# A first expert layer sorted by expert in place of one that runs every token through all eight experts, with the last gather behind the first tile's up products

## The chip, the cores and the metric

The kernel runs on one core of one Trainium2 chip. The metric is the device time of one execution in microseconds (us). A core has TensorE (PE, matrix products into the PSUM memory; PEld is its weight load), VectorE (DVE), ScalarE (ACT), GpSimd (POOL) and SyncE (SP, which issues most of the loads), and all of them use the on-chip memory SBUF. Matmul in float32 is written as two instructions in the records; `float32r` (fp32r) products are single.

## The reference, cut to what matters

A small vision tower on 16 images: a patch embedding to 36 tokens an image (576 tokens of width 192), then four pairs of a token mixer and a second layer, each on a normalised copy of the stream and added back to it. The change is in the second layer of pair 0: eight experts, one for each token.

```
x = layernorm(h).reshape(-1, 192)                  # 576 tokens
p = softmax(x @ router_w + router_b)               # 8 experts
e = argmax(p)                                      # one expert for a token
y = silu(x @ w1[e]) * (x @ w2[e])                  # 192 -> 512
h = h + max(p) * (y @ w3[e])                       # 512 -> 192
```

The order of the stages is attention 0, these experts (M0), a grid attention, attention 1, attention 2, experts M2 (8 and a shared one, top 2), attention 3, experts M3 (16, top 8).

## The kernel before

Every engine has a program of its own, written out by hand in one function; the engines meet through counted semaphores (`wait_ge`, `then_inc`). Each stage normalises the tokens in two halves of 288 (`layer_norm`, DVE; the power of the variance is on POOL), turns them on PE so that features lie on partitions (`turn`, lines 550 to 563), and copies them out of PSUM. The last turn and the last output products of a stage overlap with the first half of the next.

**The experts before.** `moe` (PE at lines 592 to 705, ACT at 1056, DVE at 1597, POOL at 1939) is shared by the three expert layers. It never gathers tokens. For M0 it goes through 8 experts x 2 halves x 4 chunks of 128 hidden features = 64 units. Products here are split: weights and tokens are each stored as a rounded high part and a low part in fp32r (`WH`, `WL`, `XH`, `XL`, and `X1`, that holds high and low of the last 64 features on the two halves of the partitions), and a unit's gate and its up product are five fp32r products each:

```
mm(o, WH[r][:, 0, w], XH[:, cols], start=True, stop=False)
mm(o, WH[r][:, 0, w], XL[:, cols], start=False, stop=False)
mm(o, WL[r][:, 0, w], XH[:, cols], start=False, stop=False)
mm(o, WH[r][:, 1, w], X1[:, cols], start=False, stop=False)
last = mm(o, WL[r][:, 1, w], X1[:, cols], start=False, stop=True)
```

ACT takes the silu of the gate, DVE multiplies by the up part, POOL multiplies by a 0/1 row that is 1 where the token belongs to the expert (`spread_both` makes these rows), ACT and DVE split the result into high and low (`AH`, `AL`), and `down` (line 649) adds five more fp32r products to a sum in PSUM. ACT (`up_high`, `down_high`) and DVE (`up_low`, `down_low`) split each expert's weights one expert ahead; those of expert 0 are split inside attention 0. Weights come through two pairs of buffers, `RG` and `RD`, that SP fills (`slots`). DVE also does `centre(n)` in this stage, twelve pieces of work on the weights of attention 1. At the end `by_tokens` turns the sums back, and `stream` adds them, times the largest probability, to `H`. `keep_clock` puts products with no use on PE while it would wait in the grid stage.

Of the kernel before, what the change touches and what calls it, by code (L numbers as in the profile page):

```python
# [33 lines left out]
NC_ = 2  # L34
CR = (128, C - 128)
CB = (CR[0], CR[1] + 1)
TP = 96
# [100 lines left out]
MOES = [M0, M2, M3]  # L138
A0.then, A1.then, A2.then, A3.then = M0, None, M2, M3
# [5 lines left out]
SG0 = {M0.name: 0, M2.name: M0.units}  # L145
AM0 = {m.name: sum(x.weighted(u) for x in MOES[:i] for u in range(x.units)) for i, m in enumerate(MOES)}
SLOTS = [(m, s) for m in MOES for s in range(m.slots)]
RING = 2
PARTS = 9
WG_ = 1024  # L150
GRP = 14
STAGES = [("attn", A0), ("moe", M0), ("grid", None), ("attn", A1), ("attn", A2), ("moe", M2), ("attn", A3), ("moe", M3)]
# [6 lines left out]
YN = [sum(1 for k, _ in STAGES[:i] if k != "moe") for i in range(len(STAGES) + 1)]  # L159
# [61 lines left out]
def bass_vit_tower(nc, t, out):  # L221
    with ExitStack() as ctx:
# [40 lines left out]
        rstd = sb("rstd", [TP, NG])  # L263
        cst = sb("cst", [128, 128])
# [40 lines left out]
        TX2 = over("TX2", [TP, TAU * 256], F32)  # L305
        WH = [sb("WH0", [128, NC_, WG_], F32R)]
        WL = [sb("WL0", [128, NC_, WG_], F32R)]
        DW = [sb("DW0", [128, 4, 2 * C], F32R)]
# [5 lines left out]
        with ExitStack() as place:  # L314
# [8 lines left out]
            TX = [sb1(f"TX{r}", [TP, TAU * 256]) for r in range(2)] + [TX2]  # L323

# [46 lines left out]
        def turned_by_time(j, c, lo, hi):  # L371

            return turned(j, c, lo, hi).rearrange("k (t b m) -> k t b m", t=TAU, b=HB)

        XH = sb("XH", [128, B * N], F32R)
# [4 lines left out]
        DW.append(sb("DW1", [128, 4, 2 * C], F32R))  # L380
        AH = [sb(f"AH{r}", [128, HN], F32R) for r in range(PARTS)]
# [17 lines left out]
            "dve_step", "pool_step",  # L399
        )}  # L400
        in_att = {n: sem("in_att_" + n) for n in ("l0a", "grid", "l1f", "l2a", "l3a")}
        in_w2 = [sem(f"in_w2_{k}") for k in range(3)]
# [59 lines left out]
        def _(sp):  # L462
# [38 lines left out]

            qkv(A0)
            proj(A0)
            slots(M0, 0, RING)
# [6 lines left out]
            slots(M0, RING, M0.slots)  # L511
            slots(M2, 0, RING)
# [34 lines left out]
        def _(pe):  # L547
# [27 lines left out]
            def router(i, e, stage, j):  # L575

                wait_xt(stage, j)
                if j == 0:
                    pe.wait_ge(S["x_split"], 2 * MOES.index(STAGES[stage][1]) + 1)
# [7 lines left out]
            def keep_clock(n, bank):  # L587

                for _ in range(n):
                    mm(PS[:, bank, 0:HN], WH[0][:, 0, 0:128], WH[0][:, 0, 128:128 + HN], start=True, stop=True)  # L590

            def moe(m, stage):
# [88 lines left out]
                for u in range(m.units + m.lag):  # L681
# [4 lines left out]
                    if u == 1:  # L686
                        if m is M3:
                            keep_clock(11, 7)
                        turn(stage, 1)
# [12 lines left out]
                if stage + 1 < len(STAGES):  # L702
                    keep_clock(14, 0)
                    turn(stage + 1, 0)
                by_tokens(1)

# [219 lines left out]
            def grid_attention(stage):  # L926
# [16 lines left out]
                for j in range(2):  # L943

                    keep_clock((27, 41)[j], 7)
# [33 lines left out]
            for i, (kind, arg) in enumerate(STAGES):  # L979
                if kind == "moe":  # L980
                    moe(arg, i)
                elif kind == "attn":
# [1092 lines left out]
```

## Time and profile before

| | us |
|---|---|
| median of 3 runs | 718.22 (717.99 to 719.23) |
| the profiled execution | 716.98 |
| its span, first to last instruction | 714.4 |
| PE busy in it | 678.0 |
| stage M0, first split product to the turn for the grid | 84.6 to 229.7 |

The trace holds one execution. Starts are microseconds from the span's first instruction. The time of an execution also holds what lies before and behind the span, 2.6 us here.

### The profile page before, as it was taken

Reading aid. Unit: us, or ns where it says so; the run is one execution under the profiler, and the core shown is the slowest. Engines: PE = TensorE matmul, PEld = TensorE weight load, DVE = VectorE, ACT = ScalarE, POOL = GpSimd, SP = SyncE. Lnnn points to the kernel's source line nnn. Section 1 sums busy time; section 2 is a strip of 40 time slices with the busy share of each in tenths; the row PEclk is TensorE's granted clock in tenths of the full one; section 3 lists DMA queues with packets and bytes.
Section 4 is the critical chain, followed back from the end, with each engine's and each line's share of the span. In section 5 each row is a group of like instructions: output and inputs, shape, how many; then the busy total and the mean of one; then the engine's idle time right before and its main releaser. Section 6 shows DMA issues by size and latency. Waiting matters only on the chain.

```text
span 714.4 us, 16229 instructions
## 1 busy us (share of the span) xinstructions
PE 678.0 (95%) x6345; PEld 616.3 (86%) x6345; DVE 486.0 (68%) x1198; ACT 366.3 (51%) x851; POOL 166.4 (23%) x164
## 2 busy tenths in 40 slices
PE   6999998999999999999999999999999998999996
PEld 6788898999998687799879998889999867889995
DVE  2658568888868882878774554677766747466785
ACT  0357454555543213588735753455454458357662
POOL 1200017444451202344122000054443120000000
PEclk9999999999999999999999999999999999899999
DMA  9932022222212000011100010212312100112000
GB/s 258 268 80 83 3 60 80 84 82 82 67 61 68 1 0 1 3 45 46 47 2 1 2 47 2 61 46 62 122 61 60 56 1 12 44 52 82 24 23 25
DMA packets 16891, 39.40 MB, mean 55 GB/s; under 512 B 3693, under 2 KB 4685, under 8 KB 16624
## 3 DMA queue, kind: packets, MB, share of 16 engines
q1 hardware_dynamic: 14840, 37.29, 17.9%
q10 hardware_dynamic: 1976, 1.08, 0.6%
q8 instruction: 50, 0.82, 0.5%
q14 instruction: 25, 0.20, 0.1%
HBM read 37.90 MB, written 0.44 MB: 54 GB/s over the span
## 4 chain that ended last, share of the span: by engine, by line
PE 73%; DVE 13%; ACT 7%; issue 5%; DMA 1%; POOL 1%; POOLq 0%; DVEq 0%; ACTq 0%; SPq 0%
PE PS L865 6%; PE PS L807 6%; PE PS L732 5%; PE PS L741 4%; PE PS L611 4%; PE PS L615 4%; PE PS L614 4%; PE PS L613 4%; PE PS L612 4%; DVE AL L1616 3%; PE PS L828 3%; PE PS L663 3%; PE PS L667 2%; PE PS L666 2%; PE PS L665 2%
## 5 line engine op out<-in xcount | busy, mean ns | idle before, releaser
L1065 ACT ACTIVATE MIX<-PS 128x288 f32<-128x288 f32 x118 | 48.4, 411 | 114.7 <-PE PS L615 114.5
L611 PE MATMUL PS<-XH,WH 128*128 128x288 f32 x284 | 86.3, 304 | 3.5 <-DVE OT L1605 1.4
L614 PE MATMUL PS<-X,WH 128*128 128x288 f32 x284 | 83.7, 295 | 0.0
L613 PE MATMUL PS<-XH,WL 128*128 128x288 f32 x284 | 83.7, 295 | 0.0
L615 PE MATMUL PS<-X,WL 128*128 128x288 f32 x284 | 83.7, 295 | 0.0
L612 PE MATMUL PS<-XL,WH 128*128 128x288 f32 x284 | 83.6, 295 | 0.0
L1927 POOL TENSOR_TENSOR rstd<-var,nhalf 96x3 f32<-96x3 f32 x18 | 17.2, 957 | 277.0 <-DVE var L1343 277.0
L1605 DVE TENSOR_TENSOR OT<-MIX,PS 128x288 f32<-128x288 f32 x94 | 42.3, 450 | 39.0 <-ACT MIX L1065 38.3
L1616 DVE TENSOR_TENSOR AL<-OT,AH 128x288 fp32r<-128x288 f32 x118 | 58.9, 507 | 3.3 <-ACT AH L1079 2.3
L1459 DVE TENSOR_TENSOR WL<-RG,WH 128x768 fp32r<-128x768 f32 (+2 forms) x46 | 57.8, 1258 | 3.5 <-ACT WH L1045 3.3
L611 PEld LDWEIGHTS PS<-XH,WH 128*128 128x128 f32 x284 | 53.5, 188 | 6.5 <-DVE OT L1605 1.9
L663 PE MATMUL PS<-AH,DW 128*128 128x288 f32 x166 | 52.3, 315 | 7.2 <-DVE AL L1616 7.0
L1949 POOL TENSOR_TENSOR OT<-OT,BIG 128x288 f32<-128x288 f32 x48 | 45.7, 964 | 51.9 <-DVE OT L1605 35.9
L612 PEld LDWEIGHTS PS<-XL,WH 128*128 128x128 f32 x284 | 53.5, 188 | 0.0
L614 PEld LDWEIGHTS PS<-X,WH 128*128 128x128 f32 x284 | 53.5, 188 | 0.0
L613 PEld LDWEIGHTS PS<-XH,WL 128*128 128x128 f32 x284 | 53.5, 188 | 0.0
L615 PEld LDWEIGHTS PS<-X,WL 128*128 128x128 f32 x284 | 53.5, 188 | 0.0
L1079 ACT ACTIVATE AH<-OT 128x288 fp32r<-128x288 f32 x118 | 50.2, 436 | 2.2 <-DVE OT L1611 2.2
L666 PE MATMUL PS<-AL,DW 128*128 128x288 f32 x166 | 49.0, 295 | 0.0
L665 PE MATMUL PS<-AH,DW 128*128 128x288 f32 x166 | 48.9, 295 | 0.0
L664 PE MATMUL PS<-AH,DW 128*128 128x288 f32 x166 | 48.9, 295 | 0.0
L667 PE MATMUL PS<-AL,DW 128*128 128x288 f32 x166 | 48.9, 295 | 0.0
(257 smaller groups left out, 1707.5 us busy)
## 6 DMA issues: line engine op xcount, KB each, us to landing
RG<-in_gu_l0f_dram SPq DMA_DIRECT2D x8, 512.0 KB, 4.3
RG<-in_gu_l0f_dram SPq DMA_DIRECT2D x16, 256.0 KB, 5.8
RG<-in_gu_l2f_dram SPq DMA_DIRECT2D x9, 384.0 KB, 3.6
RG<-in_gu_l2f_dram SPq DMA_DIRECT2D x18, 192.0 KB, 4.3
RD<-in_wd_l0f_dram SPq DMA_DIRECT2D x8, 384.0 KB, 3.3
RD<-in_wd_l2f_dram SPq DMA_DIRECT2D x9, 288.0 KB, 2.8
RD<-in_wd_l3f_dram SPq DMA_DIRECT2D x6, 384.0 KB, 3.1
BIG<-in_patch_dram SPq DMA_DIRECT2D x6, 288.0 KB, 7.7
```

The lines of the kernel that those rows point to most:

```text
L611: mm(o, WH[r][:, 0, w], XH[:, cols], start=True, stop=False)
L612: mm(o, WH[r][:, 0, w], XL[:, cols], start=False, stop=False)
L613: mm(o, WL[r][:, 0, w], XH[:, cols], start=False, stop=False)
L614: mm(o, WH[r][:, 1, w], X1[:, cols], start=False, stop=False)
L615: last = mm(o, WL[r][:, 1, w], X1[:, cols], start=False, stop=True)
L663: mm(FB(j, 0), W[:, 0:128], hi, start=first, stop=False)
L665: mm(FB(j, 1), both, hi, start=first, stop=False)
L666: mm(FB(j, 0), W[:, 0:128], lo, start=False, stop=final)
L667: mm(FB(j, 1), both, lo, start=False, stop=final).then_inc(S["w3_done"], 1)
L1079: activation(AH[I % PARTS][:, :], af(m, u), ACT.Copy).then_inc(S["ah_hi"], 1)
L1459: V.tensor_tensor(WL[r][:, part, 0:m.width], RG[r][:, part, 0:m.width], WH[r][:, part, 0:m.width].bitcast(F32), ALU.subtract).then_inc(S[" ...
L1616: V.tensor_tensor(AL[I % PARTS][:, :], af(m, u), AH[I % PARTS][:, :].bitcast(F32), ALU.subtract).then_inc(S["ah_lo"], 1)
```

## The change

The stage `("moe", M0)` becomes `("sorted", None)`. M0 goes from the list of shared expert layers, and with it the splits in attention 0. The new stage is a function of each engine:

1. The router's mask is multiplied by a triangle of ones and by ones (`ranks`), which gives each token its rank among the tokens of its expert; DVE makes a place of it (`positions`): tile e for the first 128 tokens of expert e, and one of four spare tiles (8 to 11) for what goes beyond 128. There are T0 = 12 tiles of S0 = 128 places.
2. `picked(n)` compares the places with a row 0 to 511 and gives a 0/1 matrix for each group of 96 tokens; `gather(n)` multiplies high and low parts of the tokens by it: 512 places at a time, features on partitions. Gather 0 and 1 (tiles 0 to 7) come first; gather 2 (the spare tiles) stands at `i == LATE`, behind tile 0's gate and up products.
3. For each tile: gate and up, 512 columns each, in full float32 with the weights as the moving operand; silu; product; four turns; a down product in float32.
4. `back` brings the rows to token order with 0/1 matrices (`PTT`) made on DVE, high and low parts in fp32r.
5. SP loads experts 0 to 3 into four rings ahead of attention 0's end and 4 to 7 as the rings come free. The weights of the spare tiles depend on the data: `owners` finds their expert, and POOL issues indirect loads.
6. `centre(i)` is done once a tile, and the useless products in the grid stage use `CT` instead of `WH`.

```diff
-MOES = [M0, M2, M3]
-A0.then, A1.then, A2.then, A3.then = M0, None, M2, M3
+MOES = [M2, M3]
+A0.then, A1.then, A2.then, A3.then = None, None, M2, M3
+E0, T0, S0, RING0 = 8, 12, 128, 4
+HID0 = 512
+RANKS = S0 * T0 // HID0
+GATHER = [4, 6, 0]
+LATE = 1
...
+            def expert(e):
+                r = e % RING0
+                if e >= RING0:
+                    sp.wait_ge(S["m0_up"], e - RING0 + 1)
+                sp.dma_start(GU[r], t["gu_l0f"][128 * e:128 * (e + 1), :]).then_inc(m0_in[r], 16)
+                if e >= RING0:
+                    sp.wait_ge(S["m0_down"], e - RING0 + 1)
+                sp.dma_start(WD[r], t["wd_l0f"][128 * e:128 * (e + 1), :]).then_inc(m0_in[r], 16)
...
+            for e in range(RING0, E0):
+                expert(e)
+            for r in range(RING):
+                sp.wait_ge(S["m0_up"], E0 + r + 1)
+                sp.wait_ge(S["m0_down"], E0 + r + 1)
+                slots(M2, r, r + 1)
...
+            def sorted_experts(stage):                                   # PE
+                def gather(n):
+                    for g in range(NG):
+                        pe.wait_ge(S["m0_picked"], NG * n + g + 1)
+                        for part, c in ((0, 0), (1, 0), (2, 1)):
+                            last = mm(PS[:, GATHER[n] + c, 0:HID0], XNS[:, g, 128 * part:128 * (part + 1)], PM[:, n % 2, g, :],
+                                      start=(g == 0 and part != 1), stop=(g == NG - 1 and part != 0), skip_group_check=True)
+                    last.then_inc(S["m0_gathered"], 1)
...
+                def up(i):
+                    if i < E0:
+                        pe.wait_ge(m0_in[i % RING0], 32 * (i // RING0 + 1))
+                    else:
+                        pe.wait_ge(m0_over[i - E0], 32)
+                    pe.wait_ge(S["m0_xs"], 2 * (i * S0 // HID0 + 1))
+                    if i == LATE:
+                        pe.wait_ge(S["m0_xs"], 2 * RANKS)
+                    if i >= 2:
+                        pe.wait_ge(S["m0_h"], i - 1)
+                    w = GU[i % RING0].rearrange("p (c f) -> p c f", c=2)
+                    for k in range(2):
+                        for c in range(2):
+                            last = mm(PS[:, up_bank(i) + k, 0:HID0], XS[:, c, i * S0:(i + 1) * S0], w[:, c, k * HID0:(k + 1) * HID0],
+                                      start=(c == 0), stop=(c == 1))
+                    last.then_inc(S["m0_up"], 1)
...
+                turn(stage, 1)
+                for j in range(2):
+                    router(*ROUTER["l0f"], stage, j)
+                ranks()
...
+                for n in range(RANKS - 1):
+                    gather(n)
+                for i in range(T0 + 2):
+                    if i == LATE:
+                        gather(RANKS - 1)
+                    if i < T0:
+                        up(i)
+                    if i == 0:
+                        positions()
+                    if 0 <= i - 1 < T0:
+                        turn_hidden(i - 1)
+                    if 0 <= i - 2 < T0:
+                        down(i - 2)
+                for j in range(2):
+                    back(j)
+                turn(stage + 1, 0)
...
+                for n in range(RANKS - 1):                               # ACT
+                    sorted_rows(n)
+                for i in range(T0 + 2):
+                    if i == LATE:
+                        sorted_rows(RANKS - 1)
+                    if i < T0:
+                        silu(i)
...
+                positions(view(3, 0, E0))                                # DVE
+                for n in range(RANKS):
+                    picked(n)
+                diagonals()
+                owners()
+                for i in range(T0 + 2):
+                    if i < T0:
+                        hidden(i)
+                    if 0 <= i - 2 < T0:
+                        low_out(i - 2)
...
+                            back(n)
+                    if i < T0:
+                        centre(i)
+                largest(M0, view)
...
+                if kind == "sorted":                                     # POOL
+                    for n_ in range(T0 - E0):
+                        b = (E0 + n_) % RING0
+                        if n_ == 0:
+                            pool.wait_ge(S["m0_index"], 1)
+                        pool.wait_ge(S["m0_up"], E0 - RING0 + n_ + 1)
+                        at = bass.IndirectOffsetOnAxis(ap=oidx[:, n_:n_ + 1], axis=0)
+                        G.indirect_dma_start(GU[b], None, t["gu_l0f"], at).then_inc(m0_over[n_], 16)
+                        pool.wait_ge(S["m0_down"], E0 - RING0 + n_ + 1)
+                        G.indirect_dma_start(WD[b], None, t["wd_l0f"], at).then_inc(m0_over[n_], 16)
```

`ranks` is 12 float32 products with 8 to 48 columns; `positions` on PE is 6 float32 products with 96 columns, and on DVE 11 small linked operations; `picked(n)` is 6 operations of 96 partitions x 512 and `back` on DVE one of 128 x 576; `turn_hidden` is 4 turns of 128 x 128; `down` is 4 float32 products with 192 columns; `back` on PE is 72 fp32r products with 192 columns for each half.

## Rows read from the trace of the kernel before

**Rows 1.** Windows of attention 0 and of stage M0: busy time (instructions) of each engine.
```profile
core 0: us, PE busy (x) PEld busy (x) DVE busy (x) ACT busy (x) POOL busy (x), PEclk, DMA share, GB/s
22.00:84.60 62.60, 60.91 (x888) 50.61 (x885) 39.40 (x110) 34.37 (x85) 4.34 (x3) 1.00 0.40 108
84.60:229.70 145.10, 140.97 (x1041) 136.27 (x1041) 115.79 (x256) 72.75 (x166) 62.18 (x66) 1.00 0.24 72
```

**Rows 2.** Timeline of PE around the start of stage M0: start us, us.
```profile
80.47 0.38 PE L559 MATMUL PS<-cst,XN 96*128 96x96 f32 x2
...
82.35 0.94 PE L865 MATMUL PS<-wp_l0a,OT 96*96 96x192 f32 x4
...
86.26 1.11 PE L582 MATMUL PS<-wr,XT 128*96 128x8 f32 x12
...
91.50 0.29 PE L611 MATMUL PS<-XH,WH 128*128 128x288 f32 x1
...
92.15 0.29 PE L611 MATMUL PS<-XH,WH 128*128 128x288 f32 x1
```

**Rows 3.** The chain that ended last, several stages: start us, us, what.
```profile
50.15 0.37 PE PS L838 x4
...
69.91 3.97 PE PS L865 x24
...
224.37 0.55 DVE MIX L1685
...
229.72 0.71 PE PS L559 x6
...
231.23 6.07 PE PS L939 x24
...
250.49 3.09 PE PS L957 x18
...
608.11 7.52 PE PS L865 x24
```

**Rows 4.** Timeline of VectorE and GpSimd in stage M0: start us, us.
```profile
84.62 0.56 DVE L1705 TENSOR_TENSOR H<-PS,H 96x384 f32<-96x384 f32 x1 [0.19 <-PE PS L865]
...
87.85 0.95 DVE L1350 TENSOR_SCALAR XN<-H,mv,rstd 96x192 f32<-96x192 f32 x3 [0.96 <-POOL rstd L1927]
...
94.75 0.20 DVE L1486 TENSOR_REDUCE rs<-PS 96x6 f32<-96x48 f32 x1
...
97.03 0.50 DVE L1544 MAX8 top<-rl 96x8 f32<-96x8 f32 x6
...
99.37 0.19 DVE L1562 TENSOR_SCALAR CB<-rl 96x48 fp32r<-96x48 f32 x1
...
208.12 7.17 POOL L1949 TENSOR_TENSOR OT<-OT,ACC 128x288 f32<-128x288 f32 x8 [1.01 <-DVE OT L1605]
...
211.64 0.99 DVE L1593 TENSOR_TENSOR wqkv_l1f<-wqkv_l1f,cw 65x256 f32<-65x256 f32 x1
```

**Rows 5.** Groups by form over the whole span, DVE and ACT: busy us, mean ns.
```profile
L1706 DVE TENSOR_TENSOR H<-PS,H 96x192 f32<-96x192 f32 x10 | 3.4, 344 | 0.0
...
L1593 DVE TENSOR_TENSOR wqkv_l1f<-wqkv_l1f,cw 128x256 f32<-128x256 f32 x6 | 2.6, 426 | 0.2
...
L1213 ACT ACTIVATE PT<-PS 128x432 f32<-128x432 f32 x16 | 8.3, 520 | 13.0 <-PE PS L838 13.0
```

**Rows 6.** Windows near the end of attention 3, columns as in the first group.
```profile
606.00:608.00 2.00, 1.20 (x30) 0.99 (x22) 1.90 (x6) 1.98 (x7) 0.00 (x0) 1.00 0.66 197
610.00:612.00 2.00, 2.00 (x8) 1.78 (x7) 1.78 (x6) 0.44 (x1) 0.00 (x0) 0.50 0.22 86
```

**Rows 7.** Loads: issues, KB each, median us from issue to landing.
```profile
RG<-in_gu_l0f_dram SPq DMA_DIRECT2D x16, 256.0 KB, 5.8
...
RD<-in_wd_l0f_dram SPq DMA_DIRECT2D x8, 384.0 KB, 3.3
```

**Rows 8.** A window of the start, with loads queued, columns as in the first group.
```profile
28.00:32.00 4.00, 4.00 (x24) 2.90 (x23) 3.21 (x6) 2.08 (x5) 2.15 (x1) 1.00 1.08 261
```

More of the change, by code:

```diff
@@ L148 @@
 RING = 2
+E0, T0, S0, RING0 = 8, 12, 128, 4
[3 more added lines that the diff above has]
+LATE = 1
+BLOB = dict(zip(("iota", "above", "ones", "thr", "kth", "eth", "base", "over", "slot", "part"),
+                np.cumsum([0, HID0, 128, 128, 32, 32, 32, E0, E0, T0]).tolist()))
+BLOB_W = BLOB["part"] + 1
 PARTS = 9
@@ L158 @@
 TAKEN = [2 * sum(1 for k, _ in STAGES[:i] if k == "attn") for i in range(len(STAGES) + 1)]
-YN = [sum(1 for k, _ in STAGES[:i] if k != "moe") for i in range(len(STAGES) + 1)]
+YN = [sum(1 for k, _ in STAGES[:i] if k not in ("moe", "sorted")) for i in range(len(STAGES) + 1)]
 XV_N = {"l0a": 0, "l1f": 1, "l2a": 2, "l3a": 3}
@@ L305, in bass_vit_tower @@
         TX2 = over("TX2", [TP, TAU * 256], F32)
+        GU = [RG[r][:, :, :].rearrange("p c f -> p (c f)") for r in range(RING)]
+        WD = [RD[r][:, :] for r in range(RING)]
+        GU.append(over("GU2", [128, 2 * WG_], F32)[:, :])
         WH = [sb("WH0", [128, NC_, WG_], F32R)]
+        GU.append(over("GU3", [128, 2 * WG_], F32)[:, :])
         WL = [sb("WL0", [128, NC_, WG_], F32R)]
+        WD2 = over("WD2", [128, 2, 4 * C], F32)
+        WD += [WD2[:, r, :] for r in range(2)]
         DW = [sb("DW0", [128, 4, 2 * C], F32R)]
@@ L323, in bass_vit_tower, with const0, scratch0, up_bank @@
             TX = [sb1(f"TX{r}", [TP, TAU * 256]) for r in range(2)] + [TX2]
+        XS = OT[:, 0:2 * S0 * T0].rearrange("p (c n) -> p c n", c=2)
+        HB0 = [BIG[:, r * HID0:(r + 1) * HID0] for r in range(2)]
+        HT0 = [BIG[:, 1920 + r * HID0:1920 + (r + 1) * HID0] for r in range(2)]
+        SG0B = [MIX[:, r * HID0:(r + 1) * HID0] for r in range(2)]
+        POST = XT[:, 0, :]
+        DIAG = ACC[0:TP, :, 0:TP]
+        def const0(name, n, rows=128):
+            return BIG[0:rows, 1024 + BLOB[name]:1024 + BLOB[name] + n]
+        def scratch0(o, n, rows=128):
+            return BIG[0:rows, 2944 + o:2944 + o + n]
+        POS = scratch0(176, NG * RANKS, TP).rearrange("p (n g) -> p n g", n=RANKS)
+        def up_bank(i):
+            return 2 * ((i + 1) % 2)
         def af(m, u):
@@ L577, in router @@
                 wait_xt(stage, j)
-                if j == 0:
+                if j == 0 and STAGES[stage][0] == "moe":
                     pe.wait_ge(S["x_split"], 2 * MOES.index(STAGES[stage][1]) + 1)
@@ L981, in _ @@
                     moe(arg, i)
+                elif kind == "sorted":
+                    sorted_experts(i)
                 elif kind == "attn":
@@ L1440, in second_half_in @@
                         w2_split(4 + part)
-                if a is A2:
+                if a is A2 or kind == "sorted":
                     return
@@ L1881, in _ @@
                     moe(arg, i)
+                elif kind == "sorted":
+                    sorted_experts(i)
                 elif kind == "attn":
@@ L2010, in moe, with put @@
         t["wd_" + m.name] = down.reshape(m.slots, m.chunks, 128, C).transpose(0, 2, 1, 3)
-    moe(M0, a["L0_ffn_w1"], a["L0_ffn_w2"], a["L0_ffn_w3"])
+    w = np.concatenate([a["L0_ffn_w1"], a["L0_ffn_w2"]], axis=2)
+    t["gu_l0f"] = np.concatenate([w[:, 0:128], np.concatenate([w[:, 128:C], w[:, 128:C]], axis=1)], axis=2).reshape(E0 * 128, 2 * WG_)
+    t["wd_l0f"] = a["L0_ffn_w3"].reshape(E0, 4, 128, C).transpose(0, 2, 1, 3).reshape(E0 * 128, 4 * C)
+    blob = z(128, BLOB_W)
+    def put(name, x):
+        x = np.asarray(x, f)
+        blob[:, BLOB[name]:BLOB[name] + x.shape[-1]] = x
+    put("iota", np.arange(HID0))
+    put("above", np.triu(np.ones((128, 128)), 1))
+    put("ones", np.ones(128))
+    put("thr", np.tile(S0 * np.arange(1, 5), E0))
+    put("kth", np.repeat(np.arange(4), E0))
+    put("eth", np.tile(np.arange(E0), 4))
+    put("base", S0 * np.arange(E0))
+    put("over", S0 * E0 - S0 - S0 * np.arange(E0))
+    put("slot", np.arange(128)[:, None] + S0 * np.arange(T0))
+    put("part", np.arange(128)[:, None])
+    t["m0c"] = blob
     cat = lambda w, s: np.concatenate([s[None], w]).transpose(0, 2, 1)
```

242 lines of the change are left out of this document (212 added, 30 removed).

## The prediction

> **What bounds the kernel now.** I read the stage table first. In the stage that the change rewrites (84.6 to 229.7 us, 145.1 us long) PE is busy for 140.97 us at granted clock 1.00, VectorE for 115.8, ScalarE for 72.8, and the DMA engines for 24% [rows 1]. The stage in front of it is PE's as well. So PE's own work sets this stage. It is 64 units of 15 products over 288 columns: 128 gate and up groups of five and 64 down groups of five. Five such products, each with other weights, start within 0.65 us (91.50 to 92.15), so the pace is 0.131 us a product, not the 0.29 us of one [rows 2]. 960 x 0.131 = 126 us; the rest is turns, router, spreads of weights and short waits. The chain of waits then gives the paces of the full float32 products, each of which leaves two records [rows 3]: 12 of 288 columns in 6.07 us and 9 of 192 columns in 3.09 us, 0.506 and 0.343 us each, 1.7 ns a column and 0.017 besides; so 0.886 for 512 columns.
>
> **The change removes** those 126 us and the stage's weight splits. Attention 0 loses six ACT and DVE splits too, worth nothing there: its stretch shows PE busy 60.9 of 62.6 us, so PE hides them [rows 1].
>
> **It adds a chain before the first sorted tile.** Nothing fills PE there; each link is on the path.
> 1. The half turn in front of the stage does three products fewer than before (the second-half copies are made only for the other expert stages): 80.47 to 82.35 before, now 0.71 as for the grid [rows 2, 3]. The last output product is then 1.2 us earlier: 83.4 instead of 84.6.
> 2. Residual add to normalised rows: 84.62 to 88.80, 4.2 us [rows 4]: 87.6. Turn, 0.8: 88.4.
> 3. Router, two halves of 12 records at 1.1 us [rows 2], and 0.1 to DVE: 90.7. The second half's copies (0.4 us) lie behind the first half's products.
> 4. Shift, eight-largest, mask: 0.4, and 2.5 less 0.8 for a product of hidden values in between [rows 4]: 92.8.
> 5. Rank products: 12 float32, 24 records. Router records of 8 columns take 1.11/12 = 0.09 us, so their weights set the pace; I take 0.10: 2.4, to 95.2. The low parts of the sorted rows are made on DVE meanwhile.
> 6. Eleven linked small DVE operations. A reduce over 96x48 takes 0.20 [rows 4]; 0.22 with the link: 2.4, to 97.6.
> 7. Selection matrices: 18 DVE operations of 512 columns. The nearest is the normalising operation with per-partition scalars, three of 192 columns in 0.95 us, 0.32 each [rows 4]; at one element a cycle 512 columns are 0.65. If only one scalar lets the operation go at twice that, 0.4. I take 0.65 as the row has no faster form. PE needs 3 products of 512 columns for each, 3 x 0.225 = 0.68 from the 0.131 for 288. So both engines are nearly equal, and the two early ranks end at 97.6 + 12 x 0.68 + 0.9 (the first pick and hops) = 106.7, whichever price holds.
> 8. Tile 0's products, 4 x 0.886 = 3.55 (110.2). DVE is still at the third rank (97.6 + 18 x 0.65 and 0.4 for offsets: 109.7) and the diagonals (six at 0.2, and a hop): 111.2. The product of positions is queued on PE ahead of the third gather and waits for this: 1.0 us idle, and 1.2 of work: 112.4. With picks at 0.4 this wait goes.
> 9. Third gather, 6 x 0.68 = 4.1, then ScalarE empties its two banks, 0.6 each (128x432 takes 520 ns [rows 5]), and tile 1 waits for it: 117.8. That is where this kernel puts the spare tiles' rows. Behind the waiting product on PE are tile 0's turn and down products; DVE and ScalarE have nothing else due, so 1.3 us of idle PE is the price.
>
> **Then the tiles**, PE after PE: 11 x 3.55 for up products, 12 turns of 0.45 (four of 108 columns 0.37 [rows 3]), 12 down products of 4 x 0.343 = 1.37: 60.9 us, to 178.7. A tile is 5.4 us. ScalarE needs 0.6 + 0.6 + 0.35 for it; DVE 0.7 (hidden), 0.35 (low part, 344 ns for 192 columns), 2 x 0.72 (positions back), 1.05 (one piece of centring, its long part 426 ns) = 3.5 [rows 5]. Both fit. The last tile's latency behind a table load: 1.0, to 179.7. The return: 144 products of 192 columns at 0.131 x 192/288, and 0.004 for a fixed part: 0.0915 each, 13.2 us, to 192.9. The grid stage's turn follows at once: it needs 5.3 us after the first half's sum (224.37 to 229.72 [rows 3]), and the second half's 6.6 us of products cover it. Hops between engines not yet counted: 1.0. So the turn that was at 229.7 stands at 193.9.
>
> **Two costs that this leaves out.** The clock: between 90.7 and 98 PE has 2.4 us of work in 7.3. After a stretch with PE busy 1.20 of 2.00 us the granted clock fell from 1.00 to 0.50 (2.4 to 1.2 GHz) and 24 output records took 7.52 us for 3.97 before [rows 3, 6]: 3.5 us lost. I take that here, for the gathers. Below stands nothing (no drop); above, a second drop at the wait after 116.5, 7.
>
> The spare tiles' weights: POOL issues them as indirect loads, 1024 KB up and 384 KB down. The down set of tile 8 waits for tile 4's down product, the end of one tile's time, and is needed 5.4 us later; each next one likewise, with the next tile's up set queued ahead of or behind it. On SP 384 KB land in 3.3 us and the last of an expert's up loads 5.8 us after its issue [rows 7], at some 260 GB/s when the engines are full [rows 8]; one tile's two sets, 1.44 MB, need 5.5 us at that. No row shows an indirect load. Bounds: as SP's, 0 us; or each late by its queue mate's 4 us less what is spare, about 3 us a tile, 12 in all. I take 2, nearer SP's rows.
>
> By the Trainium skill (DMA: Bandwidth & Descriptors, "Anatomy of one DMA — SWDGE (gpsimd) path") a load issued from GpSimd takes 2.0 us and its bytes at 436 GB/s; the estimate for 384 KB is then 2.9 us, near the row's 3.3, and the sum would be 2 us lower. No trace here shows such a load.
>
> **The sum.** 229.7 - 193.9 = 35.8; less 3.5 and 2: 30.3 us saved. The profiled execution took 716.98 (span 714.40): 686.7. The median of the runs is 1.24 above it: 688.
>
> **The rivals.**
> - *Clock held, loads in time.* 35.8 saved: 682.4; with fast picks another 1 less. For it: the stretch of 1.20 busy itself still stood at 1.00 [rows 6]. Against: seven microseconds at a third busy is more idle than what came before that fall.
> - *The spare loads bind.* 3 us a tile more than slack, 12: 698 in place of 688 (10 above my 2). For it: 1.44 MB in 5.4 us is the full rate [rows 8]. Against: DMA is otherwise idle (24%). A mechanism that would bring it: DVE and POOL hold each other up in SBUF. DVE's centring operation on 256 columns took 0.99 us while POOL multiplied, 426 ns on the mean of its kin [rows 4, 5], and here DVE is busy 3.5 of 5.4 us; if POOL writes its descriptors only in DVE's gaps, a load of 5 becomes 8.5, 3.1 over the slot, four times. The Trainium skill (SBUF — State Buffer, "SBUF: two separate sides") states such a rule: a VectorE operation in a two-port mode locks GpSimd out, and loads issued there starve for descriptors. The trace shows the lock for computing operations, none for a load.
> - *Slower than before.* The same loads decide: at more than 5.4 + 32.3/4 = 13.5 us from issue to landing for each of the four down sets, the 30.3 us and my 2 are gone; at 14 us, 720. Nothing in the trace is that slow at 384 KB (3.3), so it needs descriptors that are made one by one.
> - *The products are cheaper than costed*, the return bound by less than 0.09: under 680.
>
> **How the numbers follow.** Forecast 0.50 (684 to 693), clock and loads well 0.15 (680 to 684), loads bind 0.27 (693 to 708), slower 0.03, no change 0.01, under 680 0.04. To leave out no more than 2 in 10 the range goes from 680 to 701: outside are 0.04 below, about 0.08 of the load case, and 0.04. A measurement of this kernel tells 0.2% from nothing, 1.4 us: faster 0.96, same 0.01, slower 0.03.
>
> **What the profile after would show.** Right: no group of the split products before the grid; up products at 0.44 us a record; 3.55 us from one tile's first up product to its turn, and 5.4 from tile to tile; PE idle 1.3 us before tile 1's products, released by ScalarE; the granted clock at 0.50 for a few us near 98; the grid's turn near 199. Wrong: PE waiting on a DMA of the expert weights ahead of tiles 8 to 11 for more than 1 us each; a tile longer than 6 us, with DVE or ScalarE as releaser; gather slower than 0.7 us a group, bound by DVE.

## The result, and the profile after

The changed kernel took 683.81 us (median of 4 runs, 682.27 to 687.89), the kernel before 718.64 beside it (717.99 to 719.23). The ratio is 0.9524, 95% interval 0.9482 to 0.9567. In two later measurements of six runs each the changed kernel took 683.95 and 683.97 us, 0.9537 (0.9497 to 0.9577) and 0.9527 (0.9487 to 0.9567). Of the six runs of e10_mid below one is left out of its figures as slow: it took 691.24 us at a mean granted clock of 0.963, the others 675.98 to 678.71 us at 0.984 to 0.990. The profiled execution took 682.27 us, with a span of 680.5.

The windows of attention 0 and of the new stage answer to [rows 1]; columns are the span's stretch, its length, busy time (instructions) of PE, PEld, DVE, ACT and POOL, the granted clock, the DMA share and GB/s.

```profile
core 0: us, PE busy (x) PEld busy (x) DVE busy (x) ACT busy (x) POOL busy (x), PEclk, DMA share, GB/s
22.00:83.40 61.40, 59.69 (x882) 50.08 (x880) 35.89 (x105) 30.57 (x80) 4.35 (x3) 1.00 0.41 134
83.40:198.30 114.90, 102.88 (x506) 75.41 (x507) 52.20 (x172) 24.77 (x49) 9.77 (x10) 0.90 0.38 128
```

PE's work in the stage fell from 141.0 to 102.9 us, VectorE's from 115.8 to 52.2, ScalarE's from 72.8 to 24.8. But PE now has 12 us without work, where it had 4, and the mean granted clock is 0.90, where it was 1.00. The chain that ended last shows the order of the stage (start us, us, what), where [rows 3] had the split products:

```profile
81.29 2.10 PE PS L1043 x12
...
86.65 0.97 DVE XN L1586 x3
87.66 1.22 PE PS L621 x6
88.88 3.71 PE PS L644 x24
...
97.70 2.57 PE PS L792 x12
103.38 11.43 PE PS L776 x36
114.81 3.44 PE PS L818 x8
118.25 1.31 PE PS L800 x12
119.56 4.17 PE PS L776 x18
123.75 1.09 ACT OT L1254 x2
124.97 3.67 PE PS L818 x8
...
160.39 5.12 DMA RD<-in_wd_l0f_dram,oidx
...
185.36 12.96 PE PS L856 x144
```

L644 is the router, L792 the second kind of rank products, L776 a gather, L818 the up products, L800 `positions`, L856 the return. From tile 1 to the return every link is PE's but for two places: a load of the spare tiles (160.39 to 165.51), and ScalarE in front of the last down product (181.4 to 183.8), where it loads the table of its exponential (e5). PE's waits in 80 to 200 us (waited for: us in total, times, longest):

```profile
PE PS L621 <- DVE XN L1586: 4.3, 1, 4.3
PE PS L776 <- DVE PM L1945: 3.1, 1, 3.1
PE PS L785 <- DVE rl L1805: 2.4, 1, 2.4
PE PS L818 <- ACT OT L1254: 1.3, 1, 1.3
...
PE PS L841 <- ACT BIG L1241: 0.7, 1, 0.7
PE PS L818 <- DMA RD<-in_wd_l0f_dram,oidx: 0.3, 1, 0.3
```

The first three are the router's chain: normalised rows, places, mask. The fourth is the price of the gather's place. The last is the whole price of the spare tiles' loads. The windows of PE's clock (columns as above) show what the three long waits set off:

```profile
82.00:86.00 4.00, 1.38 (x9) 1.10 (x7) 2.17 (x9) 0.04 (x1) 0.23 (x1) 0.99 0.00 0
86.00:90.00 4.00, 2.34 (x15) 2.35 (x16) 2.14 (x6) 1.19 (x3) 0.61 (x1) 0.50 0.01 4
102.00:106.00 4.00, 2.62 (x6) 2.18 (x7) 3.83 (x13) 0.00 (x0) 0.00 (x0) 0.50 0.00 0
106.00:110.00 4.00, 4.00 (x11) 3.13 (x10) 1.87 (x6) 0.00 (x0) 0.00 (x0) 0.52 0.00 0
110.00:114.00 4.00, 4.00 (x20) 3.29 (x19) 3.17 (x11) 1.08 (x2) 0.00 (x0) 1.00 0.00 0
```

PE was busy 1.38 of 4 us, then the clock stood at 0.50 (1.2 GHz) through turn, router, ranks and the first 6.4 of the 11.4 us of the early gathers, 24 us long, and came back near 109.8 us, when PE had been busy without a pause from 103.4 us.

**Where the 33.9 us of the span came from.** The grid's turn stands at 198.32 for 229.72: 31.4. Later turns of PE stand at 335.99 for 366.64, at 409.94 for 440.53 and at 540.91 for 571.49, 30.6 to 30.7 earlier. The next one stands at 588.31 for 622.22, 33.9 earlier. These last 3.3 us can't be put down to the change: before, the clock fell to 0.50 at 608 us [rows 6], and in this execution it did not at the same place:

```profile
578.00:582.00 4.00, 4.00 (x27) 3.86 (x26) 3.13 (x9) 0.44 (x1) 0.00 (x0) 1.00 0.26 95
```

In e1, e4 and e10 below, whose edits all lie in the expert stage, it did fall there. Here is e4:

```profile
576.00:578.00 2.00, 2.00 (x10) 1.85 (x10) 1.97 (x5) 0.48 (x2) 0.00 (x0) 0.50 0.76 185
```

### The profile page after: what moved, and what is told of

It is laid out like the page before. It is cut to its first block, busy times and chain, and to the rows that moved or that the text cites. A ratio compares the mean times of both kernels' runs of the same rounds, so it can differ in the third digit from the quotient of the medians.

```text
span 680.5 us, 14646 instructions
## 1 busy us (share of the span) xinstructions
PE 635.9 (93%) x5793; PEld 552.9 (81%) x5793; DVE 418.6 (62%) x1109; ACT 314.5 (46%) x730; POOL 114.0 (17%) x108
## 4 chain that ended last, share of the span: by engine, by line
PE 74%; DVE 12%; ACT 7%; issue 4%; DMA 1%; POOL 1%; POOLq 0%; DVEq 0%; SPq 0%; ACTq 0%
PE PS L985 6%; PE PS L818 6%; PE PS L910 6%; PE PS L1043 6%; PE PS L919 4%; PE PS L1006 3%; PE PS L673 2%; PE PS L776 2%; PE PS L1146 2%; PE PS L1033 2%; PE PS L677 2%; PE PS L675 2%; PE PS L676 2%; PE PS L674 2%; PE PS L841 2%
## 5 line engine op out<-in xcount | busy, mean ns | idle before, releaser
L673 PE MATMUL PS<-XH,WH 128*128 128x288 f32 x156 | 48.1, 308 | 3.3 <-DVE OT L1848 1.4
L674 PE MATMUL PS<-XL,WH 128*128 128x288 f32 x156 | 46.0, 295 | 0.0
L676 PE MATMUL PS<-X,WH 128*128 128x288 f32 x156 | 46.0, 295 | 0.0
L675 PE MATMUL PS<-XH,WL 128*128 128x288 f32 x156 | 46.0, 295 | 0.0
L677 PE MATMUL PS<-X,WL 128*128 128x288 f32 x156 | 45.9, 295 | 0.0
L725 PE MATMUL PS<-AH,DW 128*128 128x288 f32 x102 | 32.0, 313 | 4.4 <-DVE AL L1859 4.2
L910 PE MATMUL PS<-wqkv_l1f,XT 128*96 128x256 f32 (+1 forms) x144 | 34.3, 387 | 0.8 <-ACT XT L1194 0.8
L1702 DVE TENSOR_TENSOR WL<-RG,WH 128x768 fp32r<-128x768 f32 (+1 forms) x30 | 31.0, 1037 | 3.4 <-ACT WH L1280 3.3
L910 PEld LDWEIGHTS PS<-wqkv_l1f,XT 128*96 128x96 f32 (+1 forms) x144 | 29.1, 209 | 2.5 <-issue 1.0
L728 PE MATMUL PS<-AL,DW 128*128 128x288 f32 x102 | 30.1, 295 | 0.0
L726 PE MATMUL PS<-AH,DW 128*128 128x288 f32 x102 | 30.1, 295 | 0.0
L727 PE MATMUL PS<-AH,DW 128*128 128x288 f32 x102 | 30.1, 295 | 0.0
L729 PE MATMUL PS<-AL,DW 128*128 128x288 f32 x102 | 30.1, 295 | 0.0
```

Source lines behind the costliest of these rows:

```text
L725: mm(FB(j, 0), W[:, 0:128], hi, start=first, stop=False)
L726: mm(FB(j, 0), W[:, 256:384], hi, start=False, stop=False)
L910: last = mm(PSF[0:TP, 1024 + tau * 2 * a.fq:1024 + (tau + 1) * 2 * a.fq], tile(XT[0:CB[c], c, 0:B * N], j, tau), W[0:CB[c], c, g * 2 * a.f ...
L1702: V.tensor_tensor(WL[r][:, part, 0:m.width], RG[r][:, part, 0:m.width], WH[r][:, part, 0:m.width].bitcast(F32), ALU.subtract).then_inc(S[" ...
```

## The experiments

A stage is measured here from the start of the half turn in front of it to the start of the grid's turn (117.6 us in the trace above). The rest is the span without it.

| run | stage | rest | time, us | what |
|---|---|---|---|---|
| after | 117.6 | 562.9 | 683.81 (4 runs) | the change |
| a0_after | 117.2 | 563.7 | 683.95 (6 runs) | the same |
| e1_late0 | 116.7 | 565.8 | 685.13 (6 runs) | last gather ahead |
| e2_first_fill | 113.7 | 566.3 | 681.77 (1 run) | one filling |
| e3_all_fill | 110.4 | 566.5 | 679.62 (6 runs) | three fillings |
| e4_pos_behind | 115.4 | 567.2 | 686.97 (6 runs) | positions behind the gather |
| e6_plain | 117.5 | 572.7 | 691.95 (1 run) | plain loads |
| e8_dve_copies | 116.3 | 567.8 | 685.83 (1 run) | copies on VectorE |
| e9_no_spare | 87.4 | 570.5 | 659.61 (1 run) | no spare tiles |
| a1_after | 117.1 | 566.0 | 683.97 (6 runs) | the same |
| e5_exp_late | 115.7 | 566.5 | 683.91 (1 run) | table load later |
| e7_all | 110.2 | 566.1 | 677.43 (6 runs) | e3, e4, e5 together |
| e10_mid | 109.2 | 567.8 | 676.88 (5 runs) | e7, fillings placed otherwise |

The column of the rest moves by 5 us without an edit there (e6 and e9: 8 to 10), so an edit in this stage is read from its stage first. What differs there between the traces is the clock, at places that no edit touched. The half turn in front of the stage starts at 79.4 to 80.6 us where the clock held until then. It starts at 81.9 to 82.6 us in the traces of a1, e2, e3, e7 and e8, where the clock stood at 0.50 for some 3.4 us from 24 or 25 us on, and at 84.0 in e6, where it did so for 7. Behind the grid's turn the clock falls to 0.50 for 2 to 7 us at two to five places (near 310 to 330, 400, 576, 672 and 682 us; in e6 near 240 as well; e9 has seven places). The three traces of the changed kernel, the same program, differ in this as well, by 3.1 us of the rest. So it changes from execution to execution, and one trace does not tell whether an edit has a share in it.

**a0_after.** The changed kernel unedited.

> The changed kernel again, on the same chip as the next three, so that they can be compared with it and not only with the kernel before. Every theory: 682 to 688 us; granted clock 0.50 from about 86 to 110 us, and the first up product at about 115.

It gave 683.95 (682.5 to 689.4). The clock was at 0.50 from 85 to 108 us, and the first up product stands at 113.1; the half turn started 1.1 us earlier than in the first trace.

**e1_late0: the place of the gather.**

```diff
-LATE = 1
+LATE = 0
```

> LATE = 0: the spare tiles' rows are gathered ahead of tile 0. Theory (PE order is what counts): the gather of 4.2 us and the 1.2 us in which ScalarE empties it lie ahead of tile 0 in place of tile 1, so the wait only moves, 0 us; but the position product then stands behind tile 0 with nothing to wait for, as before: within 0.5 us of the changed kernel. Rival (the place of the gather is what the change is worth): 1 to 4 us slower, because VectorE's third rank of matrices and the diagonals are no longer covered by tile 0's products, and are waited for.

685.13 (684.2 to 686.18), ratio to before 0.9544 (0.9512 to 0.9576), against 0.9537 (0.9497 to 0.9577) for the control. The stage is 0.5 us shorter, of which 0.3 is a wait for a spare load that the control had and this execution had not. The time is the same within the intervals; they alone would still leave room for the rival's lower end, 1 us, and the stage rules it out. Timeline of PE, three gathers in a row and then tile 0's up products:

```profile
102.75 15.26 PE L776 MATMUL PS<-PM,XNS 96*128 96x512 f32 x54 [3.13 <-DVE PM L1945]
119.28 3.67 PE L818 MATMUL PS<-RG,OT 128*128 128x512 f32 x8 [1.27 <-ACT OT L1254]
```

The wait for ScalarE's copies is the same 1.27 us, ahead of tile 0 and not of tile 1. VectorE's third rank of matrices and the diagonals, on which the rival rested, are waited for nowhere. Having the last gather behind tile 0 saves nothing as it stands: the wait only moves.

**e4_pos_behind: something between the gather and its user.** `positions` (PE) and its copy (ScalarE) go behind the last gather.

```diff
                     if i == LATE:
                         gather(RANKS - 1)
+                        positions()
                     if i < T0:
                         up(i)
-                    if i == 0:
-                        positions()
```

> The product of positions moves from behind tile 0's up products to behind the last gather, in ScalarE's order too. Theory: it then lies in the 1.2 us in which PE waits for ScalarE to empty the gather's banks; that wait goes, and the time falls by 1.0 to 1.3 us. Rival: tile 0's silu and product, and with them its turn, come behind the emptying and the copy of the positions on ScalarE (0.6 + 0.65 us), and PE waits for them instead: no change.

```profile
116.59 4.70 PE L776 MATMUL PS<-PM,XNS 96*128 96x512 f32 x18
121.12 1.47 PE L800 MATMUL PS<-ACC,BIG 96*128 96x96 f32 x12
122.55 3.67 PE L818 MATMUL PS<-RG,OT 128*128 128x512 f32 x8
```

The wait of 1.27 us is gone, and the stage is 1.7 us shorter than the control's; 0.3 of that is the control's wait for a load. The time is not: 686.97 (684.3 to 689.44), ratio 0.957 (0.9535 to 0.9606). Behind the grid's turn windows of 2 us show the clock at 0.50 for some 20 us in sum, for some 12 in the control. So the mechanism in the stage is shown, and in the whole the forecast gain of 1.0 to 1.3 us did not show: the median is 3.0 us above the control's, with intervals that overlap.

**e2_first_fill and e3_all_fill: the clock.** Useless products with `CT` in PE's waits, 30 ahead of the second half's turn, 16 ahead of the ranks, 21 behind them; e2 has the first 30 alone.

```diff
+                keep_clock(30, 7, CT)
                 turn(stage, 1)
                 for j in range(2):
                     router(*ROUTER["l0f"], stage, j)
+                keep_clock(16, 7, CT)
                 ranks()
+                keep_clock(21, 7, CT)
```

> Only the first of the three fillings: 30 products with no use while the last rows are normalised; the waits behind the router and the rank products stay empty. Theory (the clock falls in the 4.3 us wait for the normalised rows, and stays low because the rest of the chain is thin): it now falls later, near 92 to 98 us, so that the turn (0.7) and the router (2.0) are at the full clock and the ranks and early gathers are not; 2 to 3 us of the fillings' gain. Rival (once past the first wait the clock holds): all of it, first up product about 3 us earlier still.

> Products with no use are put on PE in its three waits at the start of the stage: 30 (3.9 us at the full clock) while the last rows are normalised, 16 (2.1) behind the router, 21 (2.7) behind the rank products. Theory (the clock costs about 8 us, not the 3.5 I had put): granted clock 1.00 throughout, turn 0.65 for 1.22 us, router 2.0 for 3.7, ranks 2.6 for 5.3, early gathers 8.2 for 11.4; first up product near 106, time 7 to 9 us below the changed kernel. Rival (the clock costs little, as VectorE's small operations and matrices bound the chain): less than 4 us.

In e2 the clock no longer fell at 86 us but in the next wait, behind the router:

```profile
90.00:92.00 2.00, 2.00 (x25) 1.91 (x23) 0.46 (x2) 0.49 (x2) 0.00 (x0) 1.00 0.00 0
92.00:94.00 2.00, 0.01 (x1) 0.00 (x0) 1.78 (x21) 0.00 (x0) 0.00 (x0) 0.80 0.00 0
```

From 93 to 107 us it was at 0.50. Turn and router took 0.72 and 2.13 us, the ranks as long as without a filling (2.27 and 2.71 for the two kinds), and the stage is 3.5 us shorter, a little over what was expected. So the wait for the normalised rows is what set off the first fall, and the next wait sets off one by itself.

e3 took 679.62 (677.42 to 681.89), ratio 0.947 (0.9435 to 0.9505): 4.3 us under the control on the same chip, with a stage 6.8 us shorter. The intervals overlap by 0.0008; the slowest of its six runs is 0.6 us faster than the fastest of the control's. PE's timeline in e3:

```profile
89.47 0.71 PE L621 MATMUL PS<-cst,XN 96*128 96x96 f32 x6 [0.34 <-DVE XN L1589]
90.02 2.13 PE L644 MATMUL PS<-wr,XT 128*96 128x8 f32 x24
...
94.81 1.25 PE L788 MATMUL PS<-rl,BIG 96*128 96x40 f32 x10
95.92 1.79 PE L792 MATMUL PS<-rl,BIG 96*128 96x8 f32 x12
97.56 4.27 PE L652 MATMUL PS<-CT 128*128 128x288 f32 x21
101.67 8.38 PE L776 MATMUL PS<-PM,XNS 96*128 96x512 f32 x36
```

The same 24 router records take 2.13 us for 3.90 without fillings, and the early gathers 8.38 for 11.43. From the half turn to the first gather it is 19.3 us for 22.8. Against the first trace of the changed kernel the stage is 7.2 us shorter, and 3.5 and 3.1 of them lie in these two stretches: the loss to the clock in the changed kernel is at least some 7 us.

The theory's "granted clock 1.00 throughout" did not come: the clock fell once more, at 97 us, and was back near 100.4. The filling behind the ranks took 4.27 us, not the 2.8 that 21 products need at full clock, and so it ran past its wait. VectorE began the first matrix of 0s and 1s at 100.21 us, the gather can start 0.63 us later (102.75 and 103.38 in the changed kernel), and it started at 101.67, 0.8 us late. The chain that ended last goes through the useless products themselves:

```profile
97.71 4.12 PE PS L652 x21
```

The timed gain of 4.3 us is between the theory's and the rival's bound, since the rest of the span gave 2.8 us back: the half turn of this execution starts 2.9 us later than the control's, behind the fall of the clock near 25 us that no edit touches.

**e5_exp_late: the table load.** ScalarE's exponential goes two tiles on.

```diff
-                    if i == T0 - 1:
+                    if i == T0 + 1:
                         router_exp(0, NG * E0, TP)
```

> ScalarE's exponential for the router stands two tiles later, behind the last hidden rows. Theory: the 0.7 us that PE waited for ScalarE at the last turn of hidden values was its table load of 1.3 us, ahead of the last silu; it goes, and the stage is 0.7 us shorter (116.4 to 117.0 us). Rival: the silu needs a table load of its own again or the wait belongs to the last tile's latency, and it stays at 0.5 us or more. Either way too little for one time to tell; the trace decides.

The wait of the last down products is gone: the last two tiles' 16 records follow each other, where a wait of 0.72 us for ScalarE splits them in a1_after, the control on the same chip.

```profile
179.58 2.77 PE L841 MATMUL PS<-WD,BIG 128*128 128x192 f32 x16
```

The cause is the table load, but not where the expectation has it. In the changed kernel it stands behind the last silu (179.64) and ahead of the copy of the last turned hidden values (183.17):

```profile
181.72 1.28 ACT L1371 ACT_TABLE_LOAD   x1
```

The stage is 1.5 us shorter than that control's; 0.7 is this wait, and 0.5 is a wait for the last tile's load, which this execution did not have and the control had.

**e6_plain: indirect or plain loads.** POOL's loads of the spare tiles fetch experts 0 to 3 by a fixed address.

```diff
-                        G.indirect_dma_start(GU[b], None, t["gu_l0f"], at).then_inc(m0_over[n_], 16)
+                        G.dma_start(GU[b], t["gu_l0f"][128 * n_:128 * (n_ + 1), :]).then_inc(m0_over[n_], 16)
```

(and the same for `WD[b]`).

> The spare tiles' weights come as plain loads of fixed experts from the same POOL queue at the same places, in place of indirect ones, so tokens in spare tiles get the weights of a fixed expert. Theory (indirect loads cost no more than plain ones here): landing within 0.5 us of 5.1 us after issue, no more than 0.3 us of PE waiting for them, stage length unchanged. Rival (indirect loads are what makes the down set of a tile arrive at the last moment): landing near 3.3 us, as SP's.

POOL's timeline for the second down set, first the changed kernel, then e6:

```profile
160.39 1.03 POOL L2292 DMA_INDIRECT RD<-in_wd_l0f_dram,oidx  x1 [2.90 <-PE PS L841]
```

```profile
164.25 0.55 POOL L2292 DMA_DIRECT2D RD<-in_wd_l0f_dram  x1 [4.07 <-PE PS L841]
```

The address from SBUF costs 0.4 to 0.5 us of POOL per load, and the down sets land a median 4.5 and 3.8 us after their issue (two each in `RD` and `WD`), 4.0 and 3.6 when plain. Each of the four landed 0.1 to 0.5 us sooner when plain; the second, the one that PE waited for, after 4.6 us for 5.1. So the indirect address is not what makes that set late, and the rival is refuted. The stage is as long as before the edit, 117.5: nothing hangs on it but the last 0.3 us of wait, which is gone here. The time of 691.95 is no measure of the loads: the half turn started 3.4 us later, and the rest of the span was the longest of all runs.

**e8_dve_copies: VectorE beside POOL's loads.** Four copies of 96x576 on VectorE in each of tiles 5 to 10.

```diff
+                    if 5 <= i < 11:
+                        for _ in range(4):
+                            link(V.tensor_copy(XN[:, 0:TAU, 0:C], XN[:, TAU:2 * TAU, 0:C]))
```

> VectorE makes four more copies of 96x576 from SBUF to SBUF in each of tiles 5 to 10, about 2 us of work in its slack while POOL issues the spare loads. Theory (the loads are bound by the DMA queue, not by VectorE): POOL's issue stays at 0.94 to 1.18 us, the down sets land within 0.5 us of before, PE waits under 1 us. Rival (VectorE's two-port copies keep GpSimd from writing descriptors): issues of 1.5 us and more, landings later by 1 to 3 us, PE waits 1 to 3 us for each of tiles 8 to 11.

Two of POOL's issues with the copies nearest to them:

```profile
157.77 0.94 POOL L2293 DMA_INDIRECT RG<-in_gu_l0f_dram,oidx  x1 [0.30 <-issue]
158.68 2.31 DVE L2014 COPY XN<-XN 96x576 f32<-96x576 f32 x4
...
168.03 1.29 POOL L2293 DMA_INDIRECT GU<-in_gu_l0f_dram,oidx  x1 [0.30 <-issue]
168.16 2.32 DVE L2014 COPY XN<-XN 96x576 f32<-96x576 f32 x4
```

The copies added 2.2 us to each tile. The down sets land after 4.2 and 3.8 us, and PE waits for no load in the stage, as the theory said. But the rival was hardly put to the test: the copies stand in the gaps between POOL's issues, as in the first two lines, and only one issue of eight lies beside them, the one at 168.03. It took 1.29 us, the same one of the changed kernel 1.03, and its load landed after 6.4 us, for 6.3 there. The other seven took as long as before, 0.94 to 1.18 us. So a hold-up of an issue by VectorE's work is neither shown nor refuted; what is shown is that this much more of it costs PE nothing. The Trainium skill (SBUF — State Buffer, "SBUF: two separate sides") says that a load issued from GpSimd has its descriptors held up while such float32 copies run; the 0.26 us of the one issue would agree, and its landing shows no delay. Whether these copies took both ports no row tells.

**e9_no_spare: what the spare tiles cost.** The four spare tiles are left out, with the third gather, their loads and their part of the return; tokens beyond 128 of an expert are dropped.

```diff
+TN = 8
...
-                for i in range(T0 + 2):
-                    if i == LATE:
-                        gather(RANKS - 1)
-                    if i < T0:
+                for i in range(TN + 2):
+                    if i < TN:
...
-                    for n_ in range(T0 - E0):
+                    for n_ in range(0):
```

> The four spare tiles are left out, with their gather, their loads and their part of the return; tokens beyond 128 of an expert are dropped. Theory (the stage is PE's sum of terms): 4 x 5.17 for the tiles, 4.17 + 1.25 for the gather and the emptying, 48 x 0.09 = 4.3 for the return: 30.4 us shorter. Rival (the start chain and hops bind, so that terms don't add): less than 25 us.

The stage takes 87.4 us, 30.2 less than in the first trace with them (29.8 less than in a0_after), for 30.4 expected: the terms add. Only 96 products of return remain:

```profile
157.16 8.88 PE L855 MATMUL PS<-YS,PTT 128*96 128x192 f32 x96
```

**a1_after, e7_all, e10_mid: the edits together.** The three ran on the same chip. e7 has the edits of e3, e4 and e5. e10 is e7 with

```diff
+                    keep_clock(8, 7, CT)
                     for g in range(NG):
                         last = mm(PS[:, 6, 0:E0], const0("ones", 128, TP), mask[:, g, :], start=(g == 0), stop=(g == NG - 1))
...
-                keep_clock(21, 7, CT)
+                keep_clock(17, 7, CT)
```

> The changed kernel once more, as the measure for the runs beside it: 682 to 687 us, ratio to the kernel before near 0.953. The stage from the half turn in front of it (first turn of six) to the grid's turn takes 117 to 118 us, with the granted clock at 0.50 for some 24 us of it.

> Three edits together: the useless products of 30, 16 and 21 in the stage's idle places, the product of positions moved behind the last gather, and ScalarE's exponential (a table load) moved two tiles later. My theory (what the stage lost to the clock and to two waits is separate and adds): in the stage -6.6 to -7.2 for the fillings, -1.3 to -1.7 for ScalarE's wait, -0.7 for the wait behind the table load, so the stage is 108 to 109 us for the 117.1 to 117.7 of the changed kernel, and the time 8 to 9.5 us under the changed kernel's on the same chip, near 675. Rival (the clock takes it back elsewhere): the stage is that short, but dips of the granted clock behind the grid's turn give back 3 us or more, as they did when positions were moved alone: 678 or more. Second rival (the waits only move): the stage is over 111 us.

> As the run with all three edits, but 8 of the useless products stand between the two kinds of rank products and 17 in place of 21 behind them. With 16 and 21 the granted clock went to 0.50 from 97 to 101 us, though PE was busy throughout: what stood before it were rank products of 8 columns. Theory (thin products let the clock fall, busy or not): with wider products between them there is no fall there: the gathers start 0.3 to 1.2 us earlier than in the run with 16 and 21, and the windows of 96 to 102 us show 1.00. Rival (the fall hangs on the waits before it or on the place in time): it falls all the same, and the gathers start 0.5 us or more later.

| | stage | time, us | ratio to before |
|---|---|---|---|
| a1_after | 117.1 | 683.97 (680.24 to 686.62) | 0.9527 (0.9487 to 0.9567) |
| e7_all | 110.2 | 677.43 (670.89 to 678.47) | 0.9422 (0.9378 to 0.9466) |
| e10_mid | 109.2 | 676.88 (675.98 to 678.71) | 0.9429 (0.9391 to 0.9467) |

In a1_after the clock was at 0.50 for 20.5 us and not 24, as it fell at 89 us and not at 85. e7 and e10 are faster than the changed kernel, by 6.5 and 7.1 us, and the intervals do not overlap. All waits of 80 to 200 us that e4 and e5 were to take away are gone. The rest of the span is as long as in the control (566.1 and 566.0 us), so the first rival, that the clock takes 3 us back elsewhere, did not come, nor the second, a stage over 111 us. But e7's stage is 7.0 us under the control's, not 8 to 9, and only 0.2 under e3's. The windows of e7 and, behind them, of e10 say why:

```profile
96.00:98.00 2.00, 2.00 (x12) 2.00 (x12) 0.31 (x2) 0.00 (x0) 0.00 (x0) 0.57 0.00 0
100.00:102.00 2.00, 2.00 (x10) 2.00 (x10) 1.96 (x6) 0.00 (x0) 0.00 (x0) 0.50 0.00 0
```

```profile
94.00:96.00 2.00, 2.00 (x19) 2.00 (x18) 0.00 (x0) 0.00 (x0) 0.00 (x0) 1.00 0.00 0
96.00:98.00 2.00, 2.00 (x11) 2.00 (x11) 1.09 (x6) 0.00 (x0) 0.00 (x0) 0.51 0.00 0
```

The clock was at 0.50 from 96.6 to 103 us in e7, from 97.0 to 100.4 in e3. From the half turn to the first gather it is 20.7 us in e7, 19.8 in e10, 19.3 in e3. Most of this difference is again the filling behind the ranks: it took 5.39 us in e7, where its 21 products need 2.8 at full clock. VectorE's matrices would have let the gather start at 100.8; it started at 102.66, 1.9 us late. In e10 with 17 products it is 0.4 us late.

And with eight wide products between the rank products the clock fell all the same in e10, at 96 us, for 3.4 us. The gathers start 0.8 us earlier than in e7, as the theory had it, but for another reason: the fall is shorter and the filling too. The theory that thin products alone let it fall is not borne out; what does stays open.

## Why the prediction was right, and where it was not

The forecast of 688 us was 4.2 above the median, and its mechanism held: the expert stage is PE's, the split products are gone, a chain of the router's stands unfilled in front of the tiles, and the tiles follow PE after PE. The grid's turn was forecast at 199.4 with both costs, and stands at 198.3. That closeness is luck in part. The clock cost 3.5 us more than was put for it and the rank products 0.8 more even near full clock; against them stand 2.2 us for the tiles' products, 1.7 for the spare loads, 1.0 for the wait for `diagonals`, and some smaller ones. Of the 4.4 us between the 686.7 forecast for the profiled execution and its 682.27, 3.3 are the fall of the clock near the end that this execution did not have, and 0.8 lie outside the span. The expert stage gave 1.1 us more than forecast, and 0.8 of that was gone again by the next stages.

| step | forecast | measured |
|---|---|---|
| last output product ends | 83.4 | 83.4 |
| normalised rows | 87.6 | 87.6 |
| turn, router | 0.8, 2.3 | 1.2, 3.7 (0.7, 2.0 at full clock, e3) |
| rank products | 2.4 | 5.3 (3.2 in e3, all but the last 0.7 us at full clock) |
| eleven small DVE operations | 2.4 | 2.44 |
| first pick and hops, early gathers | 0.9, 8.2 | 0.6, 11.4 (8.2 at full clock, e3) |
| tile 0, last gather | 3.55, 4.1 | 3.44, 4.17 |
| PE's wait for `diagonals` | 1.0 | 0 |
| PE's wait for ScalarE | 1.3 | 1.3 |
| from tile to tile | 5.4 | 5.17 |
| return | 13.2 | 12.96 |
| clock | 3.5 | at least some 7 |
| spare loads | 2 | 0.3 |

**The clock** is the term that was mis-sized. The prediction put a fall "for a few us near 98", behind the mask and rank waits, for 3.5 us. It fell already at 86 us, in the 4.3 us wait for the normalised rows. The prediction had seen that wait as a link of the chain, not as idle time of PE that counts for the clock, although PE is busy only 1.38 of the 4 us there. From then on thin products with waits between them did not bring it back in 17 us. The forecast's upper bound of 7 has the size that e3 measured, but by luck: it was for a second fall at the wait after 116.5 us, and that fall did not come (the clock is at 1.00 from 110 us to the end of the stage). A gather took 0.95 us a group, over the 0.7 that was named as a sign of being wrong; the clock was the cause, not VectorE.

**The picks.** The price was open between 0.65 and 0.4; the prediction took 0.65. VectorE's timeline in the changed kernel:

```profile
100.29 0.19 DVE L1925 TENSOR_TENSOR BIG<-PS,BIG 128x32 f32<-128x32 f32 x1 [4.65 <-PE PS L792]
...
102.75 2.46 DVE L1945 TENSOR_SCALAR PM<-BIG 96x512 fp32r<-96x512 f32 x6
```

Six of 512 columns in 2.46 us are 0.41 each. As the text said, the early gathers stayed PE's, and the wait for `diagonals` went: 1.0 us. The tiles' products were also a little cheaper than costed from [rows 3] (3.44 for 3.55, 1.30 for 1.37): 5.17 us from tile to tile for the 5.37 of its terms, 2.2 us over eleven.

**The spare loads** were given 2 us, with a rival of 12. The rates were the error. [rows 8] show 261 GB/s with loads queued, and by that rate the rival had the two sets of a tile fill the 5.4 us of a tile; in the changed kernel the engines moved 392 GB/s from 146 to 150 us. The down sets landed 3.8 and 4.5 us after their issue (medians), 5.1 for the second one, which is the one the chain shows. That just fits the slot, as 0.3 us of wait here and up to 0.5 in other executions show. By the Trainium skill (DMA: Bandwidth & Descriptors, "Anatomy of one DMA — SWDGE (gpsimd) path") the estimate for them was 2.9 us; the landings took 0.9 to 1.6 us longer, and the measurement decides.

**The rivals.** "Clock held" is refuted by the windows, "loads bind" by the waits (0.3 us in all, 0.5 in a1_after, for the 12 of the rival); e6 shows that indirect addresses cost half a microsecond a load, and whether VectorE can hold up an issue, the mechanism that the rival named, stays open (e8). "The products are cheaper" held for the tiles, by some 2 us, and for the return by 0.2; the time was not under 680. "Slower" had nothing.

**The place of the gather**, the part that gives this change its name, was priced at 1.3 us of idle PE. That number held, but e1 shows that the other place costs the same: no gain of either over the other shows. The wait is there because nothing stands between the gather and its user; with `positions` there it goes (e4).

## What to carry to other kernels

Where a change takes work away from the engine that was always busy, the waits that were hidden are now where its clock falls: look for the first stretch with PE mostly idle, and price every product from there to the next unbroken stretch at half clock. Fill such waits with useless products if the operands are at hand; here that returned 6.8 us in the stage and 4.3 in the time, for three lines. Size the last filling before a product that others wait for with care: if the clock falls in it, it takes up to twice as long and becomes the wait itself (0.8 us in e3, 1.9 in e7). And moving work so that a producer stands directly in front of its user in either order moves a wait and does not remove it: put independent work between them.

## What was not expected of the hardware

- The clock stayed at 0.50 for 20 to 24 us through small products with waits between them, and it fell at 96 to 97 us in e3, e7 and e10 with PE busy 1.8 to 2.0 of every 2 us in the six before. Filled waits are not enough in each case.
- Products of zeros held the clock over a wait: `CT`, which VectorE sets to zero at 1.0 us, is the operand of the fillings, and the router behind the first of them ran at 1.00 (e2, e3).
- Copies of 96x576 took VectorE 552 ns each, the compare of 128x576 with one scalar per partition 0.47 (two in 0.94).
- Short falls of the clock in stages that no edit touched move the rest of the span by 3 us between executions of one kernel and by up to 5 (10 in e6) between kernels that differ only here. A gain of 1 to 2 us in one stage (e1, e4, e5) can't be read from the time; it is read from the stage.
